# A layer of attention and experts: the last lead-in step gets its own order, and two pieces of its work go into the first attention step

## The reference

```python
x = x + attn(layernorm(x), Wqg, Wkv, Wout)
x = x + moe(layernorm(x), gate_kernel, gate_bias, w_gate, w_up, w_down, sw_gate, sw_up, sw_down)

# attn: keys of 16, values of 64 per head
queries, keys, values = l2norm(queries), l2norm(keys), l2norm(values)
attn = square(relu(einsum('bhid,bhjd->bhij', queries, keys)))
aggr = einsum('bhij,bhjd->bhid', attn, values)
out = tanh_norm(aggr) * tanh(silu(gates))          # then @ Wout
# moe: 4 of 16 experts by a grouped top-k, plus a shared expert
inter = silu(x @ w_gate[e]) * (x @ w_up[e])        # then @ w_down[e], weighted and summed
```

## Time and profile before

| | |
|---|---|
| median of 3 runs | 714.83 us (712.07, 714.83, 715.86) |
| the profiled execution | 712.51 us, of which the span of instructions is 710.5 us |
| PE busy | 665.4 us, 94% of the span |
| DVE, ACT, POOL busy | 478.0, 431.8, 352.1 us |
| mean granted clock of PE | 0.990 |
| step -2 and step -1 | up to 39.6 us, when the first scores start |
| step 0 | up to about 71 us |

### The profile page before, as it was taken

One profiled execution on the slowest core, in us unless ns is written; L12 is line 12 of the kernel. 1 busy time (PEld: TensorE's weight loads), 2 busy tenths in 40 slices (PEclk: granted clock), 3 DMA queues, 4 the chain that ended last, 5 costly groups with the idle time before them and its releaser, 6 DMA issues.

```text
span 710.5 us, 15317 instructions
## 1 busy us (share of the span) xinstructions
PE 665.4 (94%) x5160; PEld 515.8 (73%) x5160; DVE 478.0 (67%) x1771; ACT 431.8 (61%) x986; POOL 352.1 (50%) x368
## 2 busy tenths in 40 slices
PE   3689899999999999999999999999999999999977
PEld 2455567787787777778777778778777877767677
DVE  5745558676767777676767767576876767566684
ACT  3768576756566766656676775656667565644312
POOL 3348574645546464645555564555546355464200
PEclk9899999999999999999999999999999999999999
DMA  9998948290937639191855819094672909300000
GB/s 254 136 142 137 119 103 103 78 117 28 138 46 125 77 91 104 62 124 26 134 68 102 100 61 133 10 144 58 113 81 78 113 27 136 37 16 2 8 1 16
DMA packets 72829, 61.24 MB, mean 86 GB/s; under 512 B 8624, under 2 KB 72496, under 8 KB 72752
## 3 DMA queue, kind: packets, MB, share of 16 engines
q1 hardware_dynamic: 72752, 60.26, 57.3%
HBM read 41.37 MB, written 18.87 MB: 85 GB/s over the span
## 4 chain that ended last, share of the span: by engine, by line
PE 69%; ACT 12%; DVE 9%; issue 7%; POOL 2%; DMA 1%; SPq 0%; DVEq 0%; ACTq 0%; POOLq 0%
PE ps_a L539 14%; PE ps_f L395 10%; PE ps_f L479 9%; PE ps_f L458 8%; PE ps_f L396 7%; PE ps_f L397 7%; PE ps_s L507 5%; ACT sq L605 3%; PE ps_f L437 3%; ACT v L602 3%; ACT r L641 3%; DVE it L920 2%; POOL p L363 2%; PE ps_f L454 2%; DVE big L911 2%
## 5 line engine op out<-in xcount | busy, mean ns | idle before, releaser
L363 POOL TENSOR_TENSOR p<-r 128x512 f32<-128x512 f32 x256 | 260.8, 1040 | 288.7 <-ACT r L641 253.5
L641 ACT ACTIVATE r<-ps_s 128x512 f32<-128x512 f32 x256 | 142.3, 621 | 84.3 <-PE ps_s L507 79.0
L539 PE MATMUL ps_a<-p,v 128*64 128x256 f32 x1024 | 147.1, 393 | 3.5 <-POOL p L363 2.5
L539 PEld LDWEIGHTS ps_a<-p,v 128*64 128x64 f32 x1024 | 64.7, 136 | 45.3 <-POOL p L363 7.7
L633 ACT ACTIVATE it<-ps_f 128x256 f32<-128x256 f32 x144 | 55.2, 383 | 65.3 <-PE ps_f L397 54.4
L949 DVE TENSOR_TENSOR big<-ps_a,wt 128x256 f32<-128x256 f32 x128 | 54.1, 422 | 58.9 <-ACT big L650 57.2
L903 DVE TENSOR_TENSOR it<-ps_f,it 128x256 f32<-128x256 f32 x144 | 58.3, 421 | 42.3 <-ACT it L633 41.2
L479 PE MATMUL ps_f<-wdown,it 128*128 128x128 f32 x576 | 69.4, 280 | 2.8 <-DVE it L920 2.8
L479 PEld LDWEIGHTS ps_f<-wdown,it 128*128 128x128 f32 x576 | 66.8, 195 | 4.2 <-DVE it L920 3.8
L381 POOL TENSOR_TENSOR v<-v,vs 128x512 f32<-128x512 f32 x64 | 67.7, 1060 | 3.5 <-DVE vs L821 3.5
L650 ACT ACTIVATE big<-ps_a 128x256 f32<-128x256 f32 x128 | 53.5, 418 | 25.5 <-PE ps_f L437 22.9
(11 more groups left out here) (154 smaller groups left out, 1444.5 us busy)
## 6 DMA issues: line engine op xcount, KB each, us to landing
qk_rows<-qk_parts SPq DMA_DIRECT2D x16, 1024.0 KB, 4.5
qkt<-qk_rows SPq DMA_DIRECT2D x64, 256.0 KB, 9.6
qkt<-qk_rows SPq DMA_DIRECT2D x128, 128.0 KB, 9.0
x_in<-in_L_attn_tokens SPq DMA_DIRECT2D x16, 128.0 KB, 2.2
x_res<-in_L_attn_tokens SPq DMA_DIRECT2D x16, 128.0 KB, 13.6
out<-o_sb SPq DMA_DIRECT2D x16, 128.0 KB, 13.6
big<-in_L_attn_Wqg SPq DMA_DIRECT2D x1, 640.0 KB, 4.1
big<-in_L_attn_Wkv SPq DMA_DIRECT2D x1, 640.0 KB, 5.3
```

The costliest lines, as they stand in the source:

```text
L363: pool.tensor_tensor(p[h % 4][:], r[h % 2][:], r[h % 2][:], ALU.mult).then_inc(probs_done, 1)
L539: last = pe.matmul(ps_a[64 * e:64 * e + 64, 0:N], v[s % 3][:, t, h * DV:(h + 1) * DV], p[h % 4][:, t * N:(t + 1) * N], start=(t == 0), sto ...
L641: act.activation(r[h % 2][:], ps_s[h % 2][:], ACT.Relu).then_inc(relu_done, 1)
```

## The change

Step -1 gets an order of its own (ENDS[-1]), with all its jobs in slot 0: the transposition of batch 1 comes first, and the four values jobs of batch 1 are gone from it. They stand at the head of slots 0 and 1 of step 0, as jobs of stage P. DVE has a list of its own for step -1 (second_rows), and adds the squares of these values in slots 0 and 1 of step 0. The split of the expert weights goes from slots 4 (ACT) and 5 (DVE) of step -1 to the same slots of step 0. POOL takes the reciprocal root in slot 0 of step -1. The table of banks is keyed by stage as well, since step 0 now has values of two batches.

```diff
--- before.py
+++ after.py
@@ -54,6 +54,12 @@
         [("L", "v", 2), ("F", "cB", 2), ("L", "v", 3), ("F", "cB", 3), ("O", "x2T", 0), SKIP],
     ]
     ENDS = {
+        -1: [
+            [("L", "xT", 0), ("N", "ones", 0), ("P", "g", 0), ("N", "nT", 0), ("L", "qk", 0), ("P", "g", 1), ("L", "qk", 1),
+             ("P", "g", 2), ("P", "g", 3), SKIP, SKIP, SKIP],
+        ] + [[]] * (SLOTS - 1),
+        0: [FIRST + rest for FIRST, rest in zip(
+            ([("P", "v", 0), ("P", "v", 1)], [("P", "v", 2), ("P", "v", 3)]), FILL[:2])] + FILL[2:],
         B: [
             [("F", "lg", 0), ("N", "ones", 0), ("D", "y2", 0), ("N", "nT", 0), ("D", "y2", 1), ("F", "gu", 0), ("F", "gu", 1),
              ("F", "gu", 2), ("O", "rT", 0), ("F", "gu", 3), ("O", "rB", 0), ("O", "rB", 1), ("F", "gu", 4), ("O", "rB", 2),
@@ -197,7 +203,8 @@
         def place_banks(s):
 
             bank.clear()
-            bank.update({job[1:]: ps_f[n % 4] for n, job in enumerate(order(s)) if job != SKIP})
+            for n, job in enumerate(order(s)):
+                bank[job] = bank[job[1:]] = ps_f[n % 4]
 
 
         x_loaded, x_back = ([sem(f"{name}{q}") for q in range(2)] for name in ("x_loaded", "x_back"))
@@ -361,7 +368,7 @@
                             wait(pool, values_done, 8 * s + (h - 4) // 2 + 1)
                             pool.wait_ge(relu_done, 16 * s + h + 1)
                             pool.tensor_tensor(p[h % 4][:], r[h % 2][:], r[h % 2][:], ALU.mult).then_inc(probs_done, 1)
-                    if k == 1 and "L" in on:
+                    if k == (0 if at == -1 else 1) and "L" in on:
                         pool.wait_ge(ch_l, 3 * (s + 3))
                         root(rstd1, var1, rstd1_ready)
                     if k == 1 and at == FIRST_STEP:
@@ -398,7 +405,7 @@
 
             def filler(stage, kind, j, s, q, on, at):
                 b = s + OFFSET[stage]
-                ps = bank[(kind, j)]
+                ps = bank[(stage, kind, j)]
                 pb = 1 - q
                 xb = q if stage == "L" else pb
                 if at < 3 and kind in weights:
@@ -648,7 +655,7 @@
                                 act.wait_ge(w_lo, 4)
                         act.wait_ge(values_done, 8 * b + pair + 1)
                         act.activation(a2[:, pair, :], ps_a[:, 0:N], ACT.Square).then_inc(a2_done, 1)
-                    if at == -1 and k == 4:
+                    if at == 0 and k == 4:
                         expert_weights()
                     for stage, kind, j in fill(at)[k]:
                         if stage in on:
@@ -1024,6 +1031,29 @@
                     scale_hidden([3])
                     gate_up([8])
 
+                def low_x():
+                    dve.wait_ge(xh_ready, s + 3)
+                    dve.tensor_tensor(xl[q][:], bank[("xT", 0)][:, 0:N], xh[q][:].bitcast(F32), ALU.subtract)\
+                       .then_inc(read["xT"], 1)
+
+                def second_rows():
+
+                    row_stats(link_l, x_in[q], st1, mv1, var1)
+                    link_l.end()
+                    dve.wait_ge(rstd1_ready, s + 3)
+                    normed_rows(1, x_in[q], mv1, rstd1, xn, ln1_ready)
+                    head_sums(True, False, s)
+                    low_x()
+                    head_norm_roots()
+                    value_scales(link_p, s + 1, rq2[pq])
+                    link_p.end()
+                    low_parts(0, s + 2)
+                    low_parts(1, s + 2)
+
+                if at == -1:
+                    dve.wait_ge(x_loaded[q], (s + 2 - q) * 8 + 16)
+                    wait(dve, done["xT"], s + 2)
+                    return second_rows()
                 if at == B:
                     return last_heads()
                 if at == B + 1:
@@ -1031,6 +1061,9 @@
                 for k in range(SLOTS):
                     if k == 0:
                         gated_heads(k)
+                        if at == 0:
+                            sums(0, 1)
+                            sums(1, 1)
                         if F:
                             route_scores(link_f, fb)
                         if L_on:
@@ -1045,6 +1078,9 @@
                         if F:
                             route_experts(link_f, fb)
                             link_f.end()
+                        if at == 0:
+                            sums(2, 1)
+                            sums(3, 1)
                         gated_heads(k)
                         if F:
                             gate_up([0])
@@ -1088,16 +1124,14 @@
                         if O:
                             scale_heads([2])
                         if L_on:
-                            dve.wait_ge(xh_ready, s + 3)
-                            dve.tensor_tensor(xl[q][:], bank[("xT", 0)][:, 0:N], xh[q][:].bitcast(F32), ALU.subtract)\
-                               .then_inc(read["xT"], 1)
+                            low_x()
                         if O:
                             scale_heads([3])
                         if F:
                             gate_up([8])
                     if k == 5:
                         gated_heads(k)
-                        if at == -1:
+                        if at == 0:
                             expert_weights()
                             dve.wait_ge(w_lo, 7)
                         if O:
```

## The result

The changed kernel takes 721.97 us (median of 4 runs, 719.84 to 723.84), the kernel before 714.6 in the same runs: a ratio of 1.0112 (95% interval 1.0087 to 1.0138). It is 1.1% slower, clear of the noise and in the direction of the forecast. The shift is 7.4 us between the medians and 8.0 by the ratio, larger than the 5.9 of the sum, and 721.97 lies inside the range. The profiled execution took 719.84 us, with a span of 717.9, 7.4 longer than before. Lines L395 to L397 of before are L402 to L404 after; L507 is L514, L539 is L546, L641 is L648, L650 is L657, L757 is L764.

What follows compares the result with a forecast made beforehand. It took the 12 loads landing at 39.5 as the floor of the first attention, later steps running at PE's fixed pace. +2.5 (slot 1) + 3.4 (slots 4 to 7) = +5.9 us on 714.3 gave 720, range 715.5 to 724.

Steps and rivals of the forecast that it cites:

- The floor: End of step -1: first scores wait for the last of 12 loads, landing at 39.5, whatever the order.
- the 0.1 to 0.5 us that slot 0 was to gain: Slot 0 of step 0: relu starts at 40.0 to 40.4, POOL's first product at 40.7 to 41.1 instead of 41.21.
- Rival (2): First scores: the floor isn't the loads; POOL's first product at 37.8 instead of 41.21, -3.4 us, 711 at best; chance 0.06.
- The term of 2.5 us: Slot 1 of step 0: moved values queue ahead of nT and gated heads; +2.5 us, bounds 1.1 and 3.0.
- The clock: Start of step 0: after pausing from 35.6, PE restarts at 39.57 at 1.2 GHz, up to about 44.
- The term of 3.4: Slots 4 to 7 of step 0: moved expert split delays the relu of slot 7; +3.4 us, bounds 1.7 and 4.5.
- ACT's part: Slots 4 to 7: ACT's 2.2 us of experts ahead of g3 and the relus of slot 5; +1.7 us.
- The path behind it: Slots 5 to 7: subtractions of 2.02 and 2.19 delay low_parts(0) to 65.0, v0 of batch 2 to 65.7.
- one of the signs that I had listed for being wrong: Slot 5 of step 0: DVE subtractions of 1.3 us instead of 2 us.
- rival (3): Slots 1 and 6: PE waits longer and falls to 1.2 GHz, or both upper bounds hold; +8 to +11 us; chance 0.08.
- From step 1 on: Later steps: fixed pace on PE, equal in length; a delay from step 0 goes through undiminished.
- The sum: Whole kernel: +2.5 + 3.4 = +5.9 us, from 714.3 to 720.2, rounded to 720.

Runs made afterwards that it cites:

- order_b: Changed kernel's new order of step -1, but experts and batch 1 values stay there, qk0 ahead of nT, tanh spread, against the kernel before: ratio 1.0042.
- early_loads: order_b with three weight transfers (1.1 MB) issued behind the loads of batch 1 instead of ahead of the store of batch 0: ratio 1.0040.
- busy_pause: The changed kernel with 40 extra matmuls, read by nobody, on PE in its pause ahead of the first scores: ratio to before 1.0097.
- experts_only: The kernel before with only the split of the expert weights moved to slots 4 (ACT) and 5 (DVE) of step 0: ratio 1.0035.
- sub_only: The kernel before with only DVE's two expert subtractions and the bias moved to slot 5 of step 0, ACT's rounding staying: 712.59 us, one run.
- after_few: The changed kernel with loads for batch 0 cut to 2 of 8 pairs, so that output isn't the reference's: 716.73 us, one run.
- values_only: The changed kernel with the expert weights split in step -1 again, batch 1 values staying in step 0: ratio to before 1.0065.
- slot1_order: values_only with slot 1 of step 0 reordered: ones, g0, nT ahead of v2 and v3, whose sums follow the gated heads: ratio to before 1.0011.

## Why the prediction was right

**The floor.** Right: the loads release the first scores in the kernel before, in the changed one and in six more; in order_b and early_loads PE comes later, held by the bank of qk0, and in busy_pause the extra matmuls hold it. All that left step -1 turned into a longer wait of PE. The landing isn't fixed at 39.5, though: it was at 39.9 to 40.9 in all other runs with full loads, but for the two with late weights, also in experts_only and sub_only, whose queue ahead of it is that of before. That took the 0.1 to 0.5 us that slot 0 was to gain. Without the floor the new step -1 is ready at 39.4, as after_few shows, and not at 37.8: ACT's tanh were in the way, which I had put in the same list as over by 38. (The 1.01 us for a scaling, taken from the earlier trace rows, is there that of a product; POOL's four scalings took 4.04, so it does no harm.) Rival (2) priced this at 3.4 us against the kernel before; measured it is 1.8 (39.41 against 41.21), and outweighed.

**Slots 0 and 1.** The queue was as described, instruction by instruction: the row for nT was forecast to be copied by 49.7 and was at 50.3, the scores of pair 2 at 50.2 and 50.99; values of pair 1 50.6 and 51.72. The term of 2.5 us was mis-sized: measured 3.6 at the values of pair 1, of which 0.4 is the later start, and 3.8 from the first product up to slot 4. Missing was a second fall of the clock at 51 us, under which the values of pair 1 took 1.97 us instead of 1.08. It is not a necessary part of the cost: values_only and after_few, which didn't have it, cost 3.5 and 3.7. It followed PE's waits in slot 1, but the same waits were there in values_only, busy_pause and after_few without a fall at this place, so what brought it about stays open. slot1_order shows that the order makes about half of the cost, and busy_pause that the clock has some 1.5 us.

**The clock.** The mechanism was taken from the pause before, and half right: PE came to the first scores at the full clock, after 4.7 us without a matmul, and fell 0.4 us later, at 40.8, to come back at 44.2. The prediction said slow from the start, as it was in values_only and sub_only. Scores took 0.45 instead of 0.86, the matmuls of v0 and v1 0.43 as forecast. The kernel before falls in these slots too, from 43.9 to 47.3. The prediction uses the slow 3.0 us of its ones, g0 and nT, but doesn't say that this fall goes when the new one comes: the first stretch at half clock of the changed kernel stands in the place of one of the kernel before.

**Slots 4 to 7.** The term of 3.4 measured 4.6 in the changed kernel (3.9 if counted by PE), 3.9 in busy_pause, and 2.8 in experts_only, where the clock stayed full. ACT's part is right: 1.7 forecast, 1.6 measured as the difference of experts_only and sub_only. The path behind it was named wrongly: I let it go through DVE's subtractions, low_parts(0) and the bank of v0. In sub_only v0 waits 0.2 us for that, in the changed kernel nothing. What costs the other 1.2 us is that POOL's pair of products took 3.2 instead of 2.0 beside the first subtraction, and PE waited 1.5 us for the second of them. The prediction had this delay, at 1.1 us, and called it harmless, since it had PE come later still. The subtractions took 3.5 us together, not 4.2, and the first, with 1.35, gave one of the signs that I had listed for being wrong. That 3.4 lies near the measured values is therefore in part luck. PE fell to the slow clock from 68.1 to 71.5, with 0.43 instead of 0.23 for a matmul of v0. This is rival (3)'s mechanism: part of it came true along with the forecast.

**From step 1 on.** Right: the delay goes through unchanged, 8.8 us at the third store and 8.9 at 671.8.

**The sum.** 2.5 + 3.4 = 5.9 was forecast. Measured were 0.4 at the first product, 3.8 and 4.6, which make 8.8 at the third store, 0.1 more up to the tail, less 1.5 in the tail: 7.4 in the profiled executions. The 8.8 lies in rival (3)'s band, and 7.4 to 8.0 at the upper edge of the forecast's, to which the tail, a matter of one execution, helped. The two moves done singly cost 3.5 and 2.8 on their own ground; the rest, about 2 us up to 8.3, appears only with both. Some 1.1 of it goes with the stretch at half clock from 68 us (3.9 against 2.8), the other 0.8 or so with the one from 51. That these two falls account for all of it is argued from rows of single executions: no run of the changed kernel held the clock full there, and why it fell isn't shown.

## What to carry to other kernels

Before moving work out of a stage, ask what releases the end of that stage. Here 12 transfers did, and taking work out gained nothing; after the move it stood in the queue of engines that feed each other in turn. If work has to go into such a stage, its place in the list counts as much as its length: behind the short instructions that release others the same work cost half. An instruction can also cost through another engine that it slows down: here DVE's subtraction made POOL's product 1.2 us later, and PE waited for the product, not for DVE. A move's price should be worked out once more with PE at the slow clock: with both moves the changed kernel had three stretches at half clock in step 0, where the kernel before had one.

## What the runs showed of the hardware

The fall of the clock is not tied to one length of pause. In the kernel before it fell 2 us into a pause, at 26.8. In the changed kernel it was full through a pause of 4.7 us and fell 0.4 us after PE had started again. It also fell without such a pause: in the kernel before at 43.9, with waits of at most 1.1 us since 39.57, and in the changed kernel at 51.0 and 68.1, behind waits of up to 1.5 us.

The landing of the last load, issued at 25.0 to 25.2, moved between 39.5 and 40.9 from one kernel's profile to another's.

A DVE subtraction of two SBUF operands, 128x1152, took 1.35 us in values_only, where POOL was idle. In the changed kernel the first also took 1.35, and it was POOL's pair of products beside it that took 3.23 instead of 2.04; the second took 2.19, and POOL's scaling 2.15 instead of 1.04. The Trainium skill, SBUF — State Buffer, section "Who interferes with whom", has the two lock each other out for a whole instruction; these rows agree with it, the lengthened ones being 0.8 to 1.2 us longer where one instruction of the other engine takes 1.0 to 1.35.
